# Attention over keys in a six-part decoder: ScalarE copies the output product, GpSimd adds the tokens, and the feed-forward norm keeps one operation on GpSimd

## The reference

```python
x = _layernorm(x + _L0_attn_ref(x, ...))            # gated linear attention
x = _layernorm(x + _L0_xattn_ref(ctx_1024, x, ...))  # attention, softmax over the queries
x = _layernorm(x + _L0_ffn_ref(x, ...))              # quantised feed-forward, inner size 512
x = _layernorm(x + _L1_attn_ref(x, ...))             # causal attention with ALiBi, 16 heads
x = _layernorm(x + _L1_xattn_ref(x, ctx_1024, ctx_1024, mask, ...))  # masked attention, 16 heads
x = _layernorm(x + _L1_ffn_ref(x, ...))              # base product plus eight gated LoRA experts

def _layernorm(x, axis=-1, eps=1e-05):
    m = jnp.mean(x, axis=axis, keepdims=True)
    v = jnp.var(x, axis=axis, keepdims=True)
    return (x - m) / jnp.sqrt(v + eps)
```

## Time and profile before

| | us |
|---|---|
| median of 3 runs | 1632.65 (1630.13 to 1647.45) |
| the profiled execution | 1642.51 |
| its span, first to last instruction | 1640.7 |
| stage of attention over keys, its 128 slots | about 972 to 1557 of the span |
| feed-forward stage | about 789 to 976 of the span |

### The profile page before, as it was taken

The page is one execution under the profiler, slowest core; times in us unless marked ns, Lnnn a source line. Parts: engine busy times, 40 slices in busy tenths (PEclk is TensorE's granted clock), DMA queues, the critical chain, the costliest instruction groups (busy, mean ns, idle before and its releaser), DMA issues.

```text
span 1640.7 us, 62742 instructions
## 1 busy us (share of the span) xinstructions
PE 1333.8 (81%) x26424; PEld 864.7 (53%) x26438; DVE 1222.8 (75%) x2517; ACT 1009.7 (62%) x1748; POOL 790.0 (48%) x1606
## 2 busy tenths in 40 slices
PE   5787888888875767676666669999999989998897
PEld 2445555555543444444333336666666666666685
DVE  2445556555646888888788869899989999999856
ACT  2465665657564455554566667777777777777645
POOL 2334444444445677777688853333433233232133
PEclk8799899999987888887576669999999999999979
DMA  7000000000000000000000000000000000000012
GB/s 197 2 2 3 3 3 2 3 3 3 3 9 8 22 16 16 22 16 16 1 1 1 1 1 3 3 3 3 3 3 9 16 23 16 16 16 16 3 35 70
DMA packets 28665, 24.23 MB, mean 15 GB/s; under 512 B 3676, under 2 KB 23906, under 8 KB 28386
## 3 DMA queue, kind: packets, MB, share of 16 engines
q1 hardware_dynamic: 28386, 20.21, 4.5%
HBM read 15.94 MB, written 4.19 MB: 12 GB/s over the span
## 4 chain that ended last, share of the span: by engine, by line
PE 35%; issue 23%; POOL 17%; ACT 15%; DVE 10%; SPq 0%; another core or an unknown queue 0%; POOLq 0%; DMA 0%; ACTq 0%; DVEq 0%
PE keys_T L579 7%; ACT keys_pexp L664 5%; POOL gla_low L1110 4%; PE keys_E L475 3%; POOL gla_yg L1134 3%; ACT xs L307 2%; ACT keys_pT L646 2%; DVE cross_mx L340 2%; PE keys_E L518 2%; PE cross_O L878 2%; POOL gla_sq L1127 2%; PE keys_O L586 2%; PE cross_S L321 2%; PE cross_E L831 1%; PE keys_S L321 1%
## 5 line engine op out<-in xcount | busy, mean ns | idle before, releaser
L646 ACT ACTIVATE keys_pT<-keys_T 128x512 f32<-128x512 f32 x256 | 152.5, 596 | 107.1 <-PE keys_T L579 103.8
L330 POOL TENSOR_SCALAR keys_spread<-keys_kT,keys_heads 128x512 f32<-128x512 f32 x128 | 86.9, 698 | 257.6 <-ACT keys_kT L610 257.6
L340 DVE TENSOR_REDUCE keys_mx<-keys_S 128x16 f32<-128x1024 f32 x128 | 156.6, 1224 | 38.5 <-PE keys_S L545 23.6
L579 PE MATMUL keys_T<-ident_sb,keys_pexp 128*128 128x128 f32 x1024 | 165.0, 284 | 22.5 <-ACT keys_pexp L664 18.5
L579 PEld LDWEIGHTS keys_T<-ident_sb,keys_pexp 128*128 128x128 f32 x1024 | 112.9, 141 | 98.5 <-ACT keys_pexp L664 50.5
L343 DVE TENSOR_TENSOR keys_pe_in<-keys_S,keys_mx 128x1024 f32<-128x1024 f32 x128 | 156.7, 1224 | 4.4
L1566 DVE COPY_PREDICATED gla_at<-gla_node,gla_GP 128x256 f32<-128x256 int32 x128 | 64.9, 507 | 103.3 <-ACT gla_at L1423 99.9
L664 ACT ACTIVATE keys_pexp<-keys_pe_in 128x1024 f32<-128x1024 f32 x128 | 134.1, 1048 | 0.0
L699 DVE RECIPROCAL keys_rinv<-keys_O 128x128 f32<-128x128 f32 x128 | 120.5, 941 | 0.0
L946 ACT ACTIVATE cross_pexp<-cross_pe_in 128x1024 f32<-128x1024 f32 x64 | 67.4, 1053 | 73.5 <-DVE cross_pe_in L343 73.3
L1110 POOL TENSOR_TENSOR gla_low<-gla_ex,gla_kT 128x128 f32<-128x128 f32 x160 | 72.0, 482 | 80.6 <-ACT gla_ex L1414 80.6
(11 more groups left out here) (283 smaller groups left out, 3576.7 us busy)
## 6 DMA issues: line engine op xcount, KB each, us to landing
context<-in_ctx_T SPq DMA_DIRECT2D x32, 256.0 KB, 2.7
xs<-in_x SPq DMA_DIRECT2D x8, 512.0 KB, 7.4
out_x<-xs SPq DMA_DIRECT2D x16, 256.0 KB, 2.3
keys_mask_q<-keys_mask_b SPq DMA_DIRECT2D x64, 1.0 KB
keys_bias_right_f<-in_alibi_right SPq DMA_DIRECT2D x1, 512.0 KB, 3.9
ffn_w<-in_L_ffn_w_gate_T SPq DMA_DIRECT2D x1, 256.0 KB, 4.5
ffn_w<-in_L_ffn_w_up_T SPq DMA_DIRECT2D x1, 256.0 KB, 4.8
ffn_w<-in_L_ffn_w_down_T SPq DMA_DIRECT2D x1, 256.0 KB, 5.5
```

The lines of the kernel that those rows point to most:

```text
L330: nc.gpsimd.tensor_scalar(spread[:, :, :, j, :].rearrange("q t s k -> q (t s) k"), flat.rearrange("q (a k) -> q a k", k=SEQ), heads[:, j:j ...
L340: nc.vector.tensor_reduce(m, quads(S), X, ALU.max).then_inc(c["mx"], 1)
L579: last = nc.tensor.transpose(T[:, j * P:(j + 1) * P], pexp[:, t % 2, (4 * half + j) * P:(4 * half + j + 1) * P], sh.ident[:, :])
L646: nc.scalar.activation(pT[:, t % 2, 4 * half:4 * half + 4, :].rearrange("q n k -> q (n k)"), T[:, :], ACT.Copy).then_inc(c["pT"], 1)
```

## The change

In attention over keys, ScalarE copies the output product of tile m-3 out of its bank into a new buffer `taken` of two tiles; the copy stands between the second pT copy and the normalise. GpSimd adds the tokens to `taken` and writes `h`. VectorE no longer adds; its bn_stats come one slot later (tile m-4), and so do the moments on GpSimd and the normalise on ScalarE (tile m-8). The bank of the output product is free for `weigh` when the copy is done, no longer when `h` is.

In the feed-forward stage, GpSimd keeps only the power. VectorE adds epsilon behind bn_aggr, and one slot later, behind the largest value, makes the shift in one operation (-1 times mean times scale).

```diff
@@ attention_over_keys
+        taken = sb("taken", [P, 2, D])
...
         c.last = {**{n: ("sub", 2 * NT) for n in range(4)}, 4: ("v", 4 * NG), 5: ("pT", 4 * NT),
-                  6: ("h", 2 * NT), 7: ("h", 2 * NT)}
+                  6: ("taken", 2 * NT), 7: ("taken", 2 * NT)}
@@ GpSimd
             def slot(g, p, t):
-                if (n := back(g, p, t, 3, 2 * NG)) and n[2] == G - 1:
+                if (n := back(g, p, t, 4, 2 * NG)) and n[2] == G - 1:
                     pool_moments(nc, pool, sh, b, c, n[0], n[1])
-
-            return Part(early, (lambda g, p, t: None, slot), 3, groups=2 * NG, prepare=prepare)
+                if n := back(g, p, t, 3, 2 * NG):
+                    gg, p2, tt = n
+                    c.await_tile(pool, "taken", gg, tt)
+                    c.free_tile(pool, "norm", gg, tt)
+                    nc.gpsimd.tensor_tensor(b.h[:, p2, tt, :], taken[:, tt % 2, :], tokens(sh, gg, tt, 1), ALU.add) \
+                        .then_inc(c["h"], 1)
+
+            return Part(early, (lambda g, p, t: None, slot), 4, groups=2 * NG, prepare=prepare)
@@ TensorE, weigh
-                c.free_last(pe, "h", g, t, 2)
+                c.free_last(pe, "taken", g, t, 2)
@@ ScalarE
             def second(g, p, t):
                 if n := back(g, p, t, 1, 2 * NG):
                     take(*n, 1)
-                if n := back(g, p, t, 7, 2 * NG):
+                if n := back(g, p, t, 3, 2 * NG):
+                    gg, _, tt = n
+                    c.await_tile(act, "out_done", gg, tt)
+                    c.free_last(act, "h", gg, tt, 2)
+                    nc.scalar.activation(taken[:, tt % 2, :], OB[tt % 2][:, 2 * P:2 * P + D], ACT.Copy) \
+                        .then_inc(c["taken"], 1)
+                if n := back(g, p, t, 8, 2 * NG):
                     scalar_normalise(nc, act, sh, b, c, *n)
@@ VectorE
-                if n := back(g, p, t, 3, 2 * NG):
+                if n := back(g, p, t, 4, 2 * NG):
                     gg, p2, tt = n
-                    if tt == 0 and gg < NG:
-                        c.await_nth(dve, "xr", gg, 1, 1)
-                    vector_residual(nc, dve, sh, b, c, gg, p2, tt, OB[tt % 2][:, 2 * P:2 * P + D])
+                    c.await_tile(dve, "h", gg, tt)
+                    if tt == 0:
+                        c.free_group(dve, "rstd", gg, NORM_OPS)
+                    nc.vector.bn_stats(b.stats[:, p2, tt, :], b.h[:, p2, tt, :]).then_inc(c["stats"], 1)
@@ quantised_ffn, GpSimd
             def norm_scales(g, p):
-                c.await_nth(pool, "moments", g, G, G)
+                c.await_nth(pool, "rstd", g, 1, 3)
                 c.free_group(pool, "norm", g, 1)
-                nc.gpsimd.tensor_scalar(b.ve[:, p, :], b.mv[:, p, :, 1], 1.0, LN_EPS, ALU.mult, ALU.add) \
-                    .then_inc(c["rstd"], 1)
-                c.await_nth(pool, "rstd", g, 1, 4)
                 nc.gpsimd.tensor_tensor(b.rstd[:, p, :], b.ve[:, p, :], sh.neg_half[:, :], ALU.pow).then_inc(c["rstd"], 1)
-                c.await_nth(pool, "rstd", g, 2, 4)
-                nc.gpsimd.tensor_tensor(b.shift[:, p, :], b.mv[:, p, :, 0], b.rstd[:, p, :], ALU.mult) \
-                    .then_inc(c["rstd"], 1)
-                c.await_nth(pool, "rstd", g, 3, 4)
-                nc.gpsimd.tensor_scalar(b.nshift[:, p, :], b.shift[:, p, :], -1.0, 1.0, ALU.mult, ALU.mult) \
-                    .then_inc(c["rstd"], 1)
@@ quantised_ffn, VectorE
                 for t in range(G):
                     nc.vector.bn_aggr(b.mv[:, p, t, :], b.stats[:, p, t, :]).then_inc(c["moments"], 1)
+                c.await_nth(dve, "moments", g, G, G)
+                nc.vector.tensor_scalar(b.ve[:, p, :], b.mv[:, p, :, 1], LN_EPS, None, ALU.add).then_inc(c["rstd"], 1)
+
+            def shift(g, p):
+                c.await_nth(dve, "rstd", g, 2, 3)
+                nc.vector.scalar_tensor_tensor(b.nshift[:, p, :], b.mv[:, p, :, 0], -1.0, b.rstd[:, p, :],
+                                               ALU.mult, ALU.mult).then_inc(c["rstd"], 1)
...
                 if cur:
                     gate_up(*cur)
                     largest(*cur)
+                if (n := back(g, p, t, 4)) and n[2] == G - 1:
+                    shift(n[0], n[1])
                 if out:
                     residual(*out)
                     stats(*out)
```

More of the change, by code:

```diff
@@ L404, in attention_over_keys @@
               "xT_done", "xT", "k_done", "kT", "q_done", "qT", "spread", "v_done", "v", "scores", "mx", "sub", "exp",
-              "pT_done", "pT", "pv", "rinv", "oT")
+              "pT_done", "pT", "pv", "rinv", "oT", "taken")
         loads = [(dst[:, :], x[n]) for i, x in enumerate((ac, am))
@@ L664, in second @@
                     nc.scalar.activation(pexp[:, tt % 2, :], pe_in[:, tt % 2, :], ACT.Exp).then_inc(c["exp"], 1)
-            return Part(early, (first, second), 7, groups=2 * NG)
+            return Part(early, (first, second), 8, groups=2 * NG)
         @stage.on("vector")
@@ L708, in slot @@
                     vector_softmax_in(nc, dve, c, S, mx, pe_in, n[0], n[2])
-                if n := back(g, p, t, 3, 2 * NG):
+                if n := back(g, p, t, 4, 2 * NG):
                     gg, p2, tt = n
-                    if tt == 0 and gg < NG:
-                        c.await_nth(dve, "xr", gg, 1, 1)
-                    vector_residual(nc, dve, sh, b, c, gg, p2, tt, OB[tt % 2][:, 2 * P:2 * P + D])
-            return Part(lambda g, p, part: None, (lambda g, p, t: None, slot), 3, groups=2 * NG, prepare=prepare)
+                    c.await_tile(dve, "h", gg, tt)
+                    if tt == 0:
+                        c.free_group(dve, "rstd", gg, NORM_OPS)
+                    nc.vector.bn_stats(b.stats[:, p2, tt, :], b.h[:, p2, tt, :]).then_inc(c["stats"], 1)
+            return Part(lambda g, p, part: None, (lambda g, p, t: None, slot), 4, groups=2 * NG, prepare=prepare)
         return stage
@@ L1872, in normalise @@
             def normalise(g, p):
-                c.await_nth(act, "rstd", g, 4, 4)
+                c.await_nth(act, "rstd", g, 3, 3)
                 for t in range(G):
@@ L1981, in moments @@
                 c.await_tile(dve, "stats", g, G - 1)
-                c.free_group(dve, "rstd", g, 4)
+                c.free_group(dve, "rstd", g, 3)
                 for t in range(G):
                     nc.vector.bn_aggr(b.mv[:, p, t, :], b.stats[:, p, t, :]).then_inc(c["moments"], 1)
+                c.await_nth(dve, "moments", g, G, G)
[4 more added lines that the diff above has]
+                                               ALU.mult, ALU.mult).then_inc(c["rstd"], 1)
             def slot(g, p, t):
@@ L1998, in slot @@
                     moments(out[0], out[1])
-            return Part(early, (slot,), 3, parts=G, prepare=prepare)
+            return Part(early, (slot,), 4, parts=G, prepare=prepare)
         return stage
```

## The result

| | before | after |
|---|---|---|
| median, us (17 runs each) | 1640.77 | 1650.19 |
| the profiled execution, us | 1642.51 | 1648.37 |

The ratio of after to before is 1.0079, with a 95% interval of 1.0058 to 1.0101: 0.8% slower, where 0.9% was forecast. (This comparison has its own runs of the kernel before; their median lies 8 us above that of the three runs that the forecast started from. The two medians alone differ by 9.4 us, 0.6%, the low end of the interval.)

What follows compares the result with a forecast made beforehand. The prediction took a ring of TensorE's transposes and ScalarE's queue in attention over keys to bound the kernel. Copy +18.8 us less feed-forward gain 3.9 is +14.9 on 1632.65: 1647.5 us, range 1634 to 1664.

Steps and rivals of the forecast that it cites:

- The ring: Attention over keys: TensorE's transposes, ScalarE's pT copies, normalise and exp wait for each other in a closed 4.02 us loop.
- The copy at 0.16 us: Attention over keys: ScalarE's new copy delays its successor by 0.16 us, taken from a copy-normalise pair in another stage.
- the forecast 18.8: Attention over keys: cost of ScalarE's copy, 10.2 us in the masked half plus 8.6 us in the causal half.
- VectorE's share: Attention over keys: by busy shares VectorE is the engine to relieve, 16.36 us busy of 18.08 causal, 16.33 of 17.80 masked.
- Nothing for VectorE's relief: Attention over keys: dropping VectorE's residual add shortens its slot by about 0.32 us but is worth nothing now.
- nothing for GpSimd's add: Attention over keys: GpSimd's 128 token adds, 0.45 to 0.48 us each by the nearest row, cost 0.
- nothing for the second wait of the weighted sums: Attention over keys: TensorE's weighted sums, waiting for the copy, start up to 0.16 us later, with no second price.
- The feed-forward gain, 3.9 us: Feed-forward norm: moving small operations from GpSimd to VectorE gains 0.26 us a group in 15 groups, 3.9 us.
- The sign: Whole kernel, against the 1% bound: chance 0.05 faster, 0.41 same, 0.54 slower; the sum stood at 0.9% slower.

Runs made afterwards that it cites:

- the spare copy out of SBUF: Kernel before plus one unused 128x128 ScalarE copy a slot, from an SBUF constant, between second pT copy and normalise; ratio 1.0110.
- doubled bn_stats: Kernel before with VectorE's bn_stats done twice in each of the 128 slots, the second into an unread spare buffer; ratio 1.0022.
- the copy in the gap: Changed kernel with ScalarE's copy of the output product moved from behind the second pT copy to behind the first; ratio 0.9968.
- 3.5 alone: Kernel before with only the new feed-forward norm, attention over keys unchanged; ratio 0.9982, feed-forward stage 178.6 us against 182.1.
- the normalise in the gap: Kernel before with ScalarE's normalise moved from behind the second pT copy to behind the first, one slot later; ratio 0.9824.

## Why the prediction was right, and where it was not exact

**The ring.** Shown, from both sides: the same copy costs in one place and not in the other, and taking the normalise out shortens the slot.

**The copy at 0.16 us.** The row in another stage was a good witness: 0.16 us there, 0.16 us here (1416.75 to 1416.91). The real growth is 0.67 a masked group against 0.64 forecast, and 0.57 in most causal ones against 0.54. The first causal groups grew by less, which is why the stage's +18.6 us still came out next to the forecast 18.8: two small errors that offset each other. The difference has a row: the exp lasts 1.059 us on average after and 1.048 before, 0.01 us a slot, and it is in the ring. Why is not known: with the spare copy out of SBUF in the same place it stays 1.047. The Trainium skill ("ScalarE: Activation LUTs", section "What ACT_TABLE_LOAD costs") gives 186 ns plus 0.833 ns a column with an overlap of 93 ns; the estimate of 0.20 us from it fits the spare copy out of SBUF (0.20), while the real copy out of PSUM lasts 0.27 and costs 0.16.

**VectorE's share.** The prediction took VectorE for the engine to relieve by shares. By its own rows TensorE was busier in the causal group (17.57 us against 16.36) and nearly as busy in the masked one (16.12 against 16.33). The slip had no effect, as the sum was built on waits and not on shares.

**Nothing for VectorE's relief, nothing for GpSimd's add, nothing for the second wait of the weighted sums.** Right in all three: doubled bn_stats, and the copy in the gap, which keeps the add and the later statistics and ends at 0.9968. The wait of the weighted sums for `taken` was not removed by itself; the spare copy in the ring, without that wait, costs no less.

**The feed-forward gain, 3.9 us.** The stage gave 3.7 in this pair of profiles and 3.5 alone. The step was right in size, by luck in part, and wrong in some of its parts. The timeline of a group of the changed kernel that answers to the earlier trace rows:

```profile
887.59 0.38 DVE L1989 BATCH_NORM_AGGREGATE ffn_mv<-ffn_stats 128x2 f32<-128x6 f32 x4
887.72 0.69 POOL L1796 TENSOR_SCALAR ffn_hr<-ffn_hh,ffn_hs 128x512 f32<-128x512 f32 x1
887.72 0.68 ACT L1899 ACTIVATE ffn_sg<-ffn_G,ffn_gs 128x512 f32<-128x512 f32 x1
887.88 0.61 PE L1860 MATMUL ffn_OUT<-ffn_wi,ffn_hqT 128*128 128x128 bf16 x4
888.01 0.42 DVE L1991 TENSOR_SCALAR ffn_ve<-ffn_mv 128x4 f32<-128x4 f32 x1
888.28 0.63 PE L1831 MATMUL ffn_XT<-ffn_ident,ffn_xr 128*128 128x128 f16 x4
888.43 0.69 DVE L1957 TENSOR_TENSOR ffn_hh<-ffn_U,ffn_sg 128x512 f32<-128x512 f32 x1
...
888.95 0.69 ACT L1874 ACTIVATE ffn_xqT<-ffn_XT,ffn_back_off 128x512 bf16<-128x512 f16 x1 [0.55 <-PE ffn_XT L1831]
...
890.10 0.69 ACT L1899 ACTIVATE ffn_sg<-ffn_G,ffn_gs 128x512 f32<-128x512 f32 x1
...
890.42 0.15 DVE L1970 RECIPROCAL ffn_hs<-ffn_h 128x1 f32<-128x1 f32 x1
...
890.82 0.69 DVE L1957 TENSOR_TENSOR ffn_hh<-ffn_U,ffn_sg 128x512 f32<-128x512 f32 x1 [0.26 <-ACT ffn_sg L1899]
```

From bn_aggr to the reciprocal it is 2.83 us instead of 3.10: gain 0.27, forecast 0.26, and the idle 0.47 us is gone. But the way there is another one. The forecast left the first product where it was, 0.63 us behind bn_aggr; it stands at 0.84 here, as the gate and the addition end only then. It gave the shift 0.21 us ahead of the residual; the residual starts 0.07 us behind the shift (889.76 and 889.83), and the reciprocal 0.59 us behind the residual, not 0.67. The errors cancel. Then the step that I had not looked at: the next product waits 0.26 us for ScalarE's gate, and in this group, 10.65 us long (887.59 to 898.24), the gain is given back. Groups of the changed stages come in three lengths, about 10.24, 10.45 and 10.65, where the kernel before has mostly 10.67. The run with the copy in the gap had nearly all its groups at 10.24 (and 175.6 us for the stage), and its rows show what differs:

```profile
862.08 0.68 ACT L1899 ACTIVATE ffn_sg<-ffn_G,ffn_gs 128x512 f32<-128x512 f32 x1
862.16 0.38 DVE L1989 BATCH_NORM_AGGREGATE ffn_mv<-ffn_stats 128x2 f32<-128x6 f32 x4
862.24 0.40 PE L1860 MATMUL ffn_OUT<-ffn_wi,ffn_hqT 128*128 128x128 bf16 x4 [0.35 <-ACT ffn_hqT L1889]
862.47 0.53 PE L1831 MATMUL ffn_XT<-ffn_ident,ffn_xr 128*128 128x128 f16 x4
862.58 0.43 DVE L1991 TENSOR_SCALAR ffn_ve<-ffn_mv 128x4 f32<-128x4 f32 x1
862.91 0.68 DVE L1957 TENSOR_TENSOR ffn_hh<-ffn_U,ffn_sg 128x512 f32<-128x512 f32 x1
...
863.04 0.69 ACT L1874 ACTIVATE ffn_xqT<-ffn_XT,ffn_back_off 128x512 bf16<-128x512 f16 x1 [0.27 <-PE ffn_XT L1831]
...
864.26 0.68 ACT L1899 ACTIVATE ffn_sg<-ffn_G,ffn_gs 128x512 f32<-128x512 f32 x1
```

The four output matmuls last 0.40 us here and 0.61 there, and the gate comes 2.10 us after bn_aggr instead of 2.51. TensorE changes between its two clock levels inside this stage (mean granted clock about two thirds). Around bn_aggr the two groups stand at different levels. Windows of the changed kernel and of the run with the copy in the gap, columns as in the earlier trace rows:

```profile
885.50:889.30 3.80, 2.81 (x19) 1.96 (x20) 3.66 (x13) 1.62 (x3) 3.44 (x8) 0.50 0.01 2
```

```profile
860.00:862.40 2.40, 0.99 (x9) 0.50 (x10) 2.31 (x10) 0.90 (x2) 2.08 (x7) 1.00 0.00 0
```

The granted clock is 0.50 (the level of 1.2 GHz) in the one and 1.00 (2.4 GHz) in the other. So where in a group the level changes goes together with whether the group keeps its gain; the rows show the way (slower transposes, later xqT, later gate), but no run set the clock by itself. All groups at 10.65 us would have given 0.3 us and all at 10.24 6.5 us, and 3.9 us fell between them because the changed kernel has some of each. What sets the moment of the change in one kernel and not in the other stays open.

**The sign.** 1.0079 lies inside 1%; the chances had 0.54 on slower by over 1% and 0.41 on within. The sum itself had pointed just inside. The time forecast, 1647.5 us, lies closer to the measured 1650.19 than its parts deserve: it started from a median that was 8 us low.

## What to carry to other kernels

Ask of every instruction in which ring it stands, and count from one instruction to its own repetition, not busy shares: here the engine busy 90% had reserve and the one busy 73% had none. Before work is moved to a less busy engine, look for the wait in its queue that can hold it, and put it there; the same copy cost 18.6 us behind the second pT copy and nothing behind the first. Relieving VectorE brought nothing while the ring stood in front of it; loading it further began to cost only once the ring had been shortened.

## What the runs showed that was not expected

- VectorE's addition on 128x4 numbers lasted 0.42 us where its neighbour of the same shape takes 0.17. It began at 888.01, inside GpSimd's rounding (887.72 to 888.41), and ended at 888.43, with it. In most groups of the changed kernel it is 0.42 or 0.43 us, and 0.23 in the two in which it began later (835.58 against GpSimd's 835.09 to 835.78). The Trainium skill ("SBUF — State Buffer", section "Who interferes with whom") says that VectorE's tensor_scalar in a two-port mode and a GpSimd instruction lock each other out of a shared port for a whole instruction. The rows agree with it; in which mode the addition ran no row shows, and no run here took the lock away by itself. In this group the price was zero because ScalarE's gate ended at the same time (888.40). In the group at 862.16 the gate ended at 862.76 and the product started only at 862.91, behind the addition; but the next product there starts at 864.98, right behind its gate (864.94), so nothing of it was left a slot later.
- The exp lasts 1.059 us with the copy out of PSUM in the ring and 1.055 with the normalise in the gap, but 1.047 with the spare copy out of SBUF in the ring, and 1.048 in the kernel before and with the copy out of PSUM in the gap. What sets these 0.01 us stays open.
- The normalise moved to the gap gave 26 us, not 22: the slot with the transposes of x shrank from 4.02 to 3.72 us, where I had left it unchanged.
